# A tile table made in two parts, experts begun on 80 known tiles, the last group scattered in the expert stage, and a GRU stage without a loop

## What is computed

```python
x = x + _L0_gnn_ref(_layernorm(x), adj, ...)   # graph attention, one head
x = x + _L0_ffn_ref(_layernorm(x), ...)        # mixture of 8 experts, 2 of them per token, relu, hidden 512
x = x + _L1_gnn_ref(_layernorm(x), adj, ...)   # gated graph network, 3 rounds of message and GRU cell
x = x + _L1_ffn_ref(_layernorm(x), ...)        # mixture of 16 experts, 2 per token, silu(x w1) * (x w2), hidden 256
```

## Time and profile before

| | |
|---|---|
| median of 3 runs | 1223.04 us (1221.31 to 1224.47) |
| profiled execution | 1222.84 us, span 1220.7 us, mean granted clock 0.891 |
| PE busy | 987.0 us (81%) |
| PEld busy | 810.6 us (66%) |
| DVE busy | 770.1 us (63%) |
| ACT busy | 586.2 us (48%) |
| POOL busy | 583.4 us (48%) |

### The profile page before, as it was taken

How to read it: one execution, slowest core, us unless ns; L and a number is a source line. 1 busy time by engine, 2 the same in 40 slices (tenths; PEclk the granted TensorE clock), 3 DMA queues, 4 the chain that set the end, 5 groups by cost and what they waited for, 6 DMA issues and landing times. The chain is left out here.

```text
span 1220.7 us, 28230 instructions
## 1 busy us (share of the span) xinstructions
PE 987.0 (81%) x6880; PEld 810.6 (66%) x6881; DVE 770.1 (63%) x2955; ACT 586.2 (48%) x1485; POOL 583.4 (48%) x622
## 2 busy tenths in 40 slices
PE   4776774499999999199999989889952699999920
PEld 3665663499999999155555555555531699999920
DVE  4667765366666666347878878778663355555527
ACT  3777773233333343046655655556431344444425
POOL 1276677255555555201254263362445267666630
PEclk8778786699999999699999999999985799999965
DMA  9511112222222221222023032040006233333239
GB/s 230 184 49 48 46 50 74 62 72 69 69 69 70 70 70 48 61 68 70 19 87 93 11 103 84 19 146 7 30 27 89 71 96 89 93 89 93 75 110 328
DMA packets 121885, 98.73 MB, mean 81 GB/s; under 512 B 33384, under 2 KB 110824, under 8 KB 121576
## 3 DMA queue, kind: packets, MB, share of 16 engines
q1 hardware_dynamic: 101216, 61.24, 18.6%
q0 software_dynamic: 17152, 35.29, 9.0%
q10 hardware_dynamic: 3464, 1.59, 0.8%
HBM read 55.44 MB, written 42.62 MB: 80 GB/s over the span
## 5 line engine op out<-in xcount | busy, mean ns | idle before, releaser
L1554 POOL DMA_INDIRECT result<-e_y,e_ids x280 | 280.3, 1001 | 221.6 <-DVE e_y L1671 107.7
L1584 PE MATMUL e_ps_h<-e_xT,e_up_of 128*128 128x128 f32 x2240 | 276.9, 278 | 0.0
L1584 PEld LDWEIGHTS e_ps_h<-e_xT,e_up_of 128*128 128x128 f32 x2240 | 265.2, 194 | 0.0
L1599 PE MATMUL e_ps_y<-w_sb,e_hT 128*128 x1664 | 208.3, 275 | 0.0
L1599 PEld LDWEIGHTS e_ps_y<-w_sb,e_hT 128*128 128x128 f32 x1664 | 196.8, 192 | 0.2 <-issue 0.2
L664 POOL DMA_INDIRECT queue<-a_rows,a_slots x128 | 126.6, 989 | 90.4 <-issue 81.1
L394 POOL DMA_INDIRECT queue<-g_q_rows,g_q_slots x128 | 129.5, 1011 | 80.3 <-DVE g_q_gap L327 42.5
L1623 ACT ACTIVATE e_hT<-e_ps_h,b_sb 128x128 f32<-128x128 f32 x272 | 77.5, 368 | 113.3 <-PE e_ps_h L1584 113.3
L1653 DVE COPY e_up_of<-w_sb 128x512 f32 x280 | 114.4, 449 | 3.5 <-issue 0.7
L1679 DVE TENSOR_TENSOR e_hT<-e_ps_h,e_gate 128x512 f32<-128x512 f32 x72 | 49.7, 691 | 84.4 <-ACT e_gate L1632 84.3
L242 POOL TENSOR_TENSOR g_head_rstd<-g_head_vare,half_neg 128x4 f32<-128x4 f32 x16 | 16.3, 1022 | 174.2 <-DVE g_head_vare L235 174.2
(11 more groups left out here) (220 smaller groups left out, 1814.0 us busy)
## 6 DMA issues: line engine op xcount, KB each, us to landing
e_xq<-queue SPq DMA_DIRECT2D x280, 64.5 KB, 1.9
g_y<-result SPq DMA_DIRECT2D x16, 512.0 KB, 4.3
o_y<-result SPq DMA_DIRECT2D x16, 512.0 KB, 5.3
result<-e_y,e_ids POOLq DMA_INDIRECT x280, 2.2
x_res<-x SPq DMA_DIRECT2D x16, 256.0 KB, 3.8
w_sb<-w SPq DMA_DIRECT2D x2, 2048.0 KB, 11.5
w_sb<-w SPq DMA_DIRECT2D x16, 256.0 KB
out<-x_res SPq DMA_DIRECT2D x16, 256.0 KB, 4.5
```

Of the source, the lines that this page charges most:

```text
L1554: pool.indirect_dma_start(out=result, out_offset=bass.IndirectOffsetOnAxis(ap=ids[at_down.k][:, t, :].bitcast(U32), axis=0), in_=y[at_down ...
L1584: last = pe.matmul(ps_h[b][:, t, q * P:(q + 1) * P], up_of[at_up.k % 4][:, t, q * P:(q + 1) * P], xT[at_up.k % 4][:, t, :], start=True, st ...
L1599: last = pe.matmul(ps_y[b][:, t * D:(t + 1) * D], hT[at_down.k % 4][:, t, q * P:(q + 1) * P], down[:, bass.ds(e * (chunks * P) + q * P, P) ...
```

## The change

The tile table is made twice. `table_of_known` counts only whole tiles, from an earlier `carry`, and cuts at KNOWN = 80 tiles; it stands in the fourth step of group 13 in the attention stage, and in iteration 7 (of 0 to 7) of the GRU stage. The table of the rest is made in the expert stage, in steps 4, 5 and 6 on VectorE, with the probabilities in step 7 of the first one. SP writes the first part and loads the first four pairs before the block ends (`begin_experts`), having waited only for the groups up to 12 (11 in the GRU stage). The pads, the table's second part and the waits for the last landings move to SP's stream in the expert stage, which is written out in full. The last group's 8 scatters move to the start of POOL's stream there. `rows`, `slots`, `xq`, `y` and `adj` are allocated once for the whole program, and rows and slots get four buffers in the GRU stage too. SP loads the first two GRU groups at the end of the first expert stage. The GRU stage's `run_steps` has no loop (SP's own loop of loads stays), and POOL's order changes.

```diff
+KNOWN = 80
+HELD = 4
-def tile_table(v, c, b, experts_n):
...
+def whole_tiles(v, c, b, experts_n, more):
+    v.scalar_tensor_tensor(out=b.held[:], in0=c.carry[:, 0:experts_n], scalar=float(more),
+                           in1=c.region[:, 0:experts_n], op0=ALU.add, op1=ALU.subtract)
+    v.drain()
+    v.tensor_copy(b.held_i[:], b.held[:])
+    v.drain()
+    v.tensor_scalar(b.count_i[:], b.held_i[:], P.bit_length() - 1, None, ALU.arith_shift_right)
+    v.drain()
+    v.tensor_copy(b.count[:], b.count_i[:])
+    v.drain()
...
+def table_of_known(v, c, b, experts_n):
+    v.memset(b.unit[:], 1.0)
+    v.memset(b.upto[:, 0:1], 0.0)
+    whole_tiles(v, c, b, experts_n, 0)
+    sum_tiles(v, c, b, experts_n)
+    v.tensor_scalar(b.taken[:], b.upto[:], float(KNOWN), None, ALU.min)
+    find_rows(v, c, b, experts_n, 0)
+    v.drain()
+    v.tensor_tensor(b.used[:], b.taken[:, 1:experts_n + 1], b.taken[:, 0:experts_n], ALU.subtract)
...
+def begin_experts(nc, sp, c, b, queue, layer, experts_n, last):
+    write_table(sp, c, b, 0, KNOWN // PACK)
+    sp.wait_ge(b.written, 16 * 2)
+    for q in range(TURN):
+        wait_landed(sp, c, q, (last - q) // TURN + 1)
+    for s in range(0, HELD, 2):
+        first, second = load_pairs(nc, sp, c, queue, layer, experts_n, s)
+        load_pair(sp, c, queue, layer, s, first)
+        load_pair(sp, c, queue, layer, s + 1, second)
```

In the attention stage:

```diff
 (SP)
             sp.wait_ge(next_loaded, 16 * len(weights))
-            pad_queues(sp, c, table, c.queue0, E0, 0)
-            wait_table(sp, table, E0)
-
-            for b in range(TURN):
-                wait_landed(sp, c, b, NG // TURN)
+            begin_experts(nc, sp, c, table, c.queue0, 0, E0, NG - 4)
 (POOL)
-                if g4:
+                if g4 and not (type(g4.s) is int and g4.s == NG - 1):
 (VectorE)
+                if g3 and type(g3.s) is int and g3.s == NG - 3:
+                    wait(v, VK, "carried", NG - 4)
+                    table_of_known(v, c, table, E0)
...
-            tile_table(v, c, table, E0)
-            v.wait_ge(gap_exp, 1)
...
 (ACT)
             staged(act, body)
-            pad_queues(act, c, table, c.queue0, E0, 1)
-            write_table(act, c, table, E0)
             act.wait_ge(product_made, 1)
```

In the GRU stage:

```diff
 def run_steps(eng, body):
-            body(-1, True, False, False)
-            body(0, True, True, False)
-            body(1, True, True, True)
-            with eng.Fori(2, pairs - 1) as n:
-                body(n, True, True, True)
-            body(pairs - 1, False, True, True)
-            body(pairs, False, False, True)
+            for n in range(-1, pairs + 1):
+                body(n, n + 1 < pairs, 0 <= n < pairs, n >= 1)
 (POOL)
+                ahead = 2 if has_run else 5
+                late_rows(0, ahead)
                 if has_tail:
                     rstd_and_shift(pool, c, tail_norm, VT, GT, AT0, group(n - 1, 0))
+                late_rows(ahead, 7)
                 if has_tail:
                     rstd_and_shift(pool, c, tail_norm, VT, GT, AT0, group(n - 1, 1))
+                late_rows(7, 8)
...
-                if has_tail and not has_run:
-                    queue_rows(pool, c, r, VK, AT1, c.queue1, group(n - 1, 1))
 (ACT and VectorE, before a group's rows are written)
-                if type(at.s) is not int or at.s >= 2:
-                    wait_landed(act, c, at.b, at.half)
+                if at.s >= TURN:
+                    wait_landed(act, c, at.s % TURN, at.s // TURN)
 (VectorE)
+                    if k == 2 and n == pairs - 1:
+                        wait(v, VK, "carried", NG - 5)
+                        table_of_known(v, c, table, E1)
```

In the expert stages:

```diff
 (all engines but SP: steps)
             for k in range(UNROLL):
                 step(0, k)
-            with eng.Fori(1, pairs // UNROLL) as i:
+                if between:
+                    between(k)
+            with eng.Fori(1, known // UNROLL) as i:
+                for k in range(UNROLL):
+                    step(i, k)
+            if words:
+                eng.wait_ge(table.written, 16 * 4)
+            with eng.Fori(known // UNROLL, pairs // UNROLL) as i:
 (SP)
+            for s in range(HELD, pairs, 2):
+                if s == known:
+                    sp.wait_ge(table.padded, 16 * (experts_n + 1))
+                    sp.wait_ge(table.written, 16 * 4)
+                    for q in range(TURN):
+                        if q >= 2:
+                            wait_landed(sp, c, q, 0)
+                rows = load_pairs(nc, sp, c, queue, layer, experts_n, s)
+                for p in (s, s + 1):
+                    sp.wait_ge(ids_copied, p - HELD + 1)
+                    alone(sp, c)
+                    load_pair(sp, c, queue, layer, p, rows[p - s])
+                if s == 6:
+                    pad_rest(sp, c, table, queue, experts_n)
+                if s >= 8 and s - 8 < experts_n:
+                    sp.wait_ge(table.carry_made, 1)
+                    pad_one(nc, sp, c, table, queue, s - 8)
+                    pad_one(nc, sp, c, table, queue, s - 7)
+                if s == 28:
+                    write_table(sp, c, table, 1, words_of(experts_n) - KNOWN // PACK)
+            if layer == 0:
+                for t in range(PAIR):
+                    for k in range(UNROLL):
+                        sp.wait_ge(sent[t][k], before[t][k] + sent_of[k])
+                for at in (At(0, 0), At(0, 1)):
+                    load_group(sp, c, next_adj, at)
 (POOL)
-                        if t and not (type(at_down.s) is int and at_down.s + down_lag - up_lag + 1 >= pairs):
-                            pool.wait_ge(h_made, at_down.s + (down_lag - up_lag + 2))
...
+            for group in late:
+                queue_rows(pool, c, queue, group % TURN)
+            for q in range(2):
+                wait_landed(pool, c, q, 0)
             steps(pool, body)
 (VectorE)
+            def between(k):
+                if k == 4:
+                    table_of_rest_1(v, c, table, experts_n)
+                if k == 5:
+                    table_of_rest_2(v, c, table, experts_n)
+                if k == 6:
+                    find_rows(v, c, table, experts_n, 1)
+                if k == 7 and layer == 0:
...
```

348 lines of the change are left out of this document (170 added, 178 removed).

## The result

The changed kernel takes 1177.43 us (1176.72 to 1181.93, 4 runs) against 1223.76 us (1221.31 to 1226.93) for the kernel before: a ratio of 0.9628, 95% interval 0.9595 to 0.9661. The forecast was 1177.8. Single executions 13% or more above the others of their kernel are left out of the times in this document. The profiled execution took 1176.72 (span 1175.0), 46.1 us less than the 1222.84 from which the sum was made. That the total is right does not yet say that its terms are.

The account below looks back on a forecast made before the run. TensorE fills the expert stages, so time can move only between stages and in the GRU stage: 13.4 + 13.3 + 3.5 + 16.0 - 1.2 = 45.0 us off 1222.84 gives 1177.8 us, range 1170 to 1193.

Parts of the forecast that it names:

- Attention to experts, 13.4: Attention stage's end: 10.1 us of scatters gone, 2.6 from a faster start, 0.7 from transposes; 13.4 us gained.
- I take 0: Attention stage: VectorE's earlier table delays POOL's group 14 by at most 1.4 us; charged as 0.
- The moved scatter, 0: Expert stages' start: POOL's 8 moved scatters (10.1 us) stay hidden, with cover of 4 and some 2 us; cost nothing.
- GRU to experts, 13.3: GRU stage's end: 10.1 us of scatters, TensorE 0.7 instead of 3.2 us after the drain, 0.7 of transposes; 13.3 us.
- Experts to GRU, 3.5: Between first expert stage and GRU stage: SP issues the first loads at about 499.3 instead of 502.80; 3.5 us gained.
- the loads stay the later of the two: GRU stage's start: first loads arrive at 504.8, after VectorE's memsets and bias end at about 504.1.
- GRU stage, 16.0: GRU iterations 2 to 7: of 19.7 us lost, 1.9 of wait and 1.8 for the second power stay; 16.0 us gained.
- Of the six waits' 16.9 us, 6 x 2.5 = 15.0 go: GRU iterations 2 to 7: two late scatters, not four, before the first power remove 15.0 us of TensorE's `tok` waits.
- I charge 0.3 us each: GRU stage: five scatters before the second power make it 1.2 us later; slack takes most, 0.3 us charged each.
- keeps half its loss: Rival, GRU stage: VectorE and the second power limit next, so half the loss stays; price 8 us, 1186 us; chance 0.16.
- The table on VectorE, 1.2: GRU iteration 7 and expert stages: VectorE's table work costs 0.7 + 2 x 0.25 = 1.2 us; bounds 0 and 4.
- SP and the split loop, 0: Expert stages: SP's pads and loads take 4.7 us per two pairs, under 5.80 and 7.58; cost zero, bounds 0 and 3.

Follow-up runs that it names:

- 2, 4, 2: The changed kernel with POOL's GRU order 2 late scatters, power, 4, power, 2 instead of 2, power, 5, power, 1; 1173.65 us, ratio 0.9591 to the kernel before.
- the run with 16: The changed kernel with 16 scatters moved to each expert stage's start, new POOL orders and one pad a turn; 1165.38 us, ratio 0.9534 to the kernel before.
- the first experiment: The kernel before with only POOL's new order in the GRU stage, keeping two row buffers and the loop; 1239.16 us against 1222.03, ratio 1.0135.

## Why the prediction was right, step by step

**Attention to experts, 13.4.** Its size was right (12.7 us to the first matmul), its parts only nearly, and with luck. POOL gave 9.6 and not 10.1, the drain behind it 0.7 more than nothing, the start 2.4 and not 2.6. The step that failed is "I take 0" for the earlier table. VectorE makes it from 179.05 to 182.9, group 13's slots come 12.8 us after those of group 12 (191.61) where they came 8.2 us after before, and POOL starves 2.84 us. I had argued from group 14 alone (slots at 199.75, wanted at 203.1); the group behind the table is 13, and it was the one that was late. The loss is hidden in this execution, since its groups ran 2.7 us ahead of those of before (178.83 against 181.49 at group 12). It wasn't hidden in the three other profiles whose first expert matmul comes at 221.6 to 223.4: in the one with 2, 4, 2 group 12's slots are at 184.76. With 223.4 in place of 217.4 this part would have given 6.7 us and the total some 1183 us, within the range still. The forecast to the microsecond owes that to the execution.

**The moved scatter, 0.** Right. The eight ran in 954 to 1244 ns, median 970, beside VectorE's copies; the first result left 13.0 and 11.2 us after the first matmul (14.2 and 12.5 before). The Trainium skill ("SBUF — State Buffer", "Who interferes with whom") lets a two-port VectorE copy and a GpSimd operation block each other fully. The longest of the eight stands 0.3 us over the median, so the trace shows no block longer than that; in which mode these copies ran no row shows. The cover was 2.6 and 0.3 us, not 4 and 2, and the run with 16 shows what follows once it is used up.

**GRU to experts, 13.3.** Too small for this pair of traces, and not by the change: the stretch gave 18.0 where 15.1 stood. Iteration 7 gave 3.1 (2.5 forecast). From the start of VectorE's last addition of h (909.24 before, 877.70 after) to POOL's last scatter it is 36.80 before and 26.07 after: 10.7, of which 10.1 are the eight scatters, so the five late ones cost nothing. VectorE no longer waits 5.94 us for group 13's landing (920.10 before), but it waits 5.09 us for TensorE's scores there instead. From the last scatter to the first matmul it is 8.97 and 4.80: 4.2 us instead of 2.5. The difference is POOL's drain: behind the end of the last scatter it took 4.8 us before (947.0 to 951.8) and 3.1 after (904.73 to 907.9). That is not the number of scatters. The kernel before without the loop has the same sixteen at this place, and its drain ends 2.6 us behind them; with the new order alone it is 2.9 (964.6 to 967.5):

```profile
942.29 0.96 POOL L394 DMA_INDIRECT queue<-g_q_rows,g_q_slots  x1 [0.30 <-issue]
```

```profile
L974 POOLq DRAIN  x1: 14660/14660/14660, 931.2 to 931.2; - x1
```

So some 1.7 us of the 18.0 are a long drain in the one trace of before. They are no gain of the edit.

**Experts to GRU, 3.5.** The size was nearly right, 4.3 measured, and 3.4 to 3.6 when undone. Its reason was not: "the loads stay the later of the two". VectorE's memsets now run from 489.05 to the addition at 490.07 without a wait for a load, so VectorE's own preparation ends last.

**GRU stage, 16.0.** Here two errors met. "Of the six waits' 16.9 us, 6 x 2.5 = 15.0 go" was a little high: 13.9 of 16.9 went, and the clock with them. "I charge 0.3 us each" for the second power was the mis-sized term: seven waits, 6.1 us, show, and taking one scatter out of the five gave 5.6 us in five iterations, so 1.1 us each. Iterations 2 to 6 gained 10.1 instead of 12.8. A sentence of the same part was plainly wrong: "The four row buffers take the landing waits off VectorE and ScalarE; they gain nothing beyond that, as both have slack." With the new order they are worth 20.6 us in the five iterations, since the last scatter leaves behind the shift. It did no harm, as order and buffers came together; a forecast for the order alone would have been off by some 30 us and of the wrong sign. The rival "keeps half its loss" lay nearer than its 0.16 says: 5.8 of 15.9 us were kept (232.38 - 5 x 45.31), for the reason it gave, the five scatters ahead of the second power. The periods are 46.5 us, outside the 45.3 to 46 that the prediction asked for.

**The table on VectorE, 1.2.** Not seen where it was charged. Iteration 7 lost nothing by it (3.1 gained where 2.5 stood), and TensorE is busy 250.00 of the 250 us from 222 to 472. In the attention stage, where it was charged at nothing, it made POOL wait, though this execution's end did not show it.

**SP and the split loop, 0.** Wrong by 1.4 us in the second stage: TensorE's wait for `xq` at 928.66 is the marker that the text named. SP issues two pads in 1.5 us, then four loads in 2.5 to 3.2, with register loads between them; its turns are 5.3 and 6.1 us long at 922.87, 928.20 and 934.34, against the 5.80 of two pairs. So 4.7 us, made of issue times alone, left out a fifth of the turn. That SP's turns are why the second expert stage gained nothing is only argued: the run with 2, 4, 2 has the same SP code, turns of 4.8 to 5.8 us, no wait for `xq` and 217.86 us to the last result scatter, 0.9 less; the run with one pad a turn did not settle it.

Sum: 0.8 + 0.8 + 0.1 - 2.7 + 2.9 - 0.5 - 0.7 = 0.7 us from 45.0. The single errors are three to four times that, and one of the two largest is the long drain of before, so they cancel by luck.

## What to carry to other kernels

An order of work and the number of buffers are one edit: an item moved behind a step is also a landing that moves behind it, and the question is who overwrites that buffer next. Price each against the other before splitting them: over five iterations the order alone cost 14.4 us here, and with four buffers and no loop it gained 10.1. Where a late item is moved past one consumer, count what now stands ahead of the next one (2, 5, 1 left 1.1 us an iteration, 2, 4, 2 next to none). And when work is taken off the engine that ends a stage, ask which engine it was hiding: POOL's backlog of scatters had covered how late the last groups' slots come, and VectorE's table with them. And take a boundary's length from more than one trace: 1.7 us of a drain, and 6 us of the attention stage, came and went here with the same code.

## What the runs showed of the hardware

A stand of TensorE can cost twice, and its length alone does not say when. In the first experiment each stand at the second transposes (2.8 to 3.8 us) was followed by matmuls at half pace, 1.91 instead of 1.02 us for two of 512 columns, and each of the five windows shows 0.93. In the kernel before, stands of 3.30 and 3.29 us at `tok` (iterations 4 and 5) left the windows at 1.00, like the 2.50 us of the earlier trace rows, while one of 2.48 us in iteration 2 was followed by eight matmuls in 1.99 us, and its window shows 0.97:

```profile
626.89 1.99 PE L1134 MATMUL g_ps_n<-g_edges,g_tok 128*128 128x128 f32 x8 [2.48 <-ACT g_tok L1235]
```

```profile
724.03 1.16 PE L1134 MATMUL g_ps_n<-g_edges,g_tok 128*128 128x128 f32 x8 [3.30 <-ACT g_tok L1235]
```

What else decides it was not found.

The attention stage takes different times with the same code. With the eight scatters moved, the first expert matmul comes at 217.4 and 216.6 in two profiles, at 223.4 and 223.3 in two others, and at 221.6 with sixteen moved; before, when POOL scattered almost without a gap to the end, it was 230.1, 229.5 and 229.8. Between 100 and 150 us the granted clock is 0.82 and 0.83 in the first two, 0.70 to 0.71 in the next three, 0.78 to 0.79 in the last three. Which is cause and which effect stays open. It is as large as the effect of most edits here, so those were read in their own stage.

POOL's drain at a block's end is no fixed price: it ended 2.6 to 4.8 us behind the last scatter in the profiles read here, and 9.2 us, at both stage ends, in the fastest kernel, where nothing that the trace shows was left to wait for.
